# Rows of 1024 bytes in place of 520 in the expert queue of a transformer block

## The reference

```python
mod = (_silu(L0_c) @ L0_wmod).reshape(L0_c.shape[0], 6, 1, -1)
sa, ca, ga, sb, cb, gb = ...                       # ga, gb: sign kept, size at least 0.25
h = _layernorm(x) * (1 + ca) + sa
x = x + ga * attention(h, ...)                     # 16 heads, low-rank q/k/v, rope, causal
h = _layernorm(x) * (1 + cb) + sb
normed = _rmsnorm(h, norm_weight)
probs = softmax(normed @ router_weight.T)          # 8 experts
topk_w, topk_idx = jax.lax.top_k(probs, 2)         # weights divided by their sum
for e in range(8):
    gate, up = split(normed @ gate_up_weight[e].T) # 352 each
    moe_out += combine[..., e, None] * ((silu(gate) * up) @ down_weight[e].T)
x = x + gb * (h + alpha * moe_out)
```

## Time and profile before

| | |
|---|---|
| Median of 3 runs | 481.54 us (478.94 to 485.37) |
| The profiled execution | 481.55 us, span 479.7 us |
| Busy: TensorE, VectorE, ScalarE, POOL | 77%, 65%, 55%, 51% of the span |
| Bytes moved | 59.20 MB, 123 GB/s over the span |
| First stage | until about 271 us |
| Between the stages | about 271 to 285 us |
| 71 blocks | about 285 to 447 us |
| End | about 447 to 480 us |

### The profile page before, as it was taken

One profiled execution on the slowest core, in us unless ns is written; L12 is line 12 of the kernel. 1 busy time (PEld: TensorE's weight loads), 2 busy tenths in 40 slices (PEclk: granted clock), 3 DMA queues, 4 the chain that ended last, 5 costly groups with the idle time before them and its releaser, 6 DMA issues.

```text
span 479.7 us, 12085 instructions
## 1 busy us (share of the span) xinstructions
PE 368.7 (77%) x3935; PEld 300.4 (63%) x3936; DVE 310.2 (65%) x928; ACT 265.9 (55%) x467; POOL 245.1 (51%) x306
## 2 busy tenths in 40 slices
PE   3718899988897998988874119999999999999000
PEld 1416666665565656655552118999999999999000
DVE  2606899987788988988995714555454544454293
ACT  1326787876677877766662125656565565565000
POOL 3010346675577666866878721444444444344363
PEclk9967999997999899999986559999999999999655
DMA  8365656656656566665860033221221221211493
GB/s 267 74 138 143 161 145 160 173 155 155 145 122 142 153 164 154 160 154 149 266 264 33 29 100 103 65 65 51 69 55 51 66 64 42 65 52 50 120 305 105
DMA packets 56014, 59.20 MB, mean 123 GB/s; under 512 B 7167, under 2 KB 48128, under 8 KB 55712
## 3 DMA queue, kind: packets, MB, share of 16 engines
q1 hardware_dynamic: 51648, 50.15, 40.6%
q0 software_dynamic: 4320, 8.47, 5.3%
HBM read 34.81 MB, written 24.23 MB: 123 GB/s over the span
## 4 chain that ended last, share of the span: by engine, by line
PE 41%; SPq 19%; DVE 12%; DMA 11%; issue 8%; POOL 4%; another core or an unknown queue 3%; ACT 2%; POOLq 0%; DVEq 0%; ACTq 0%
PE SC L626 21%; DMA qdram<-rope 6%; SPq L366 5%; PE FB L640 5%; PE BK L640 5%; SPq L346 3%; SPq L361 3%; SPq L376 3%; PE SC L477 2%; POOL queue L1111 2%; SPq L369 2%; PE OB L499 2%; DVE pt L1038 2%; DVE pt L846 2%
## 5 line engine op out<-in xcount | busy, mean ns | idle before, releaser
L1131 POOL DMA_INDIRECT ydram<-ysb,xb x71 | 69.7, 982 | 98.5 <-DVE ysb L1024 97.2
L659 ACT ACTIVATE pt<-SC 128x1536 f32<-128x1536 f32 x64 | 92.6, 1447 | 43.6 <-PE SC L477 27.2
L626 PE MATMUL SC<-xTs,wgu 128*128 128x128 f32 x852 | 109.6, 279 | 3.9 <-issue 2.6
L626 PEld LDWEIGHTS SC<-xTs,wgu 128*128 128x128 f32 x852 | 102.0, 194 | 5.9 <-issue 5.7
L846 DVE SCALAR_TENSOR_TENSOR pt<-pt,cst 128x1024 f32<-128x1024 f32 x64 | 78.7, 1229 | 14.8 <-ACT pt L659 14.6
L477 PE MATMUL SC<-stq,stk 24*128 24x256 f32 (+1 forms) x1024 | 65.0, 364 | 26.7 <-ACT pt L659 14.8
L1111 POOL DMA_INDIRECT queue<-pl,dest x64 | 69.6, 1088 | 21.0 <-issue 20.2
L477 PEld LDWEIGHTS SC<-stq,stk 24*128 24x128 f32 x1024 | 50.0, 195 | 42.8 <-issue 18.2
L760 ACT ACTIVATE wgu<-gu,ws 128x704 f32 x71 | 62.1, 875 | 19.3 <-issue 19.1
L767 ACT ACTIVATE sg<-SC 128x384 f32<-128x384 f32 x71 | 34.8, 490 | 60.2 <-PE SC L626 53.6
L499 PE MATMUL OB<-pt,va 128*32 128x256 f32 (+1 forms) x1024 | 62.8, 350 | 5.4 <-DVE pt L848 3.1
(11 more groups left out here) (148 smaller groups left out, 590.8 us busy)
## 6 DMA issues: line engine op xcount, KB each, us to landing
stk<-kdram SPq DMA_DIRECT2D x64, 96.0 KB
stq<-qdram SPq DMA_DIRECT2D x64, 96.0 KB
xb<-queue SPq DMA_DIRECT2D x71, 65.0 KB
kdram<-rope SPq DMA_DIRECT2D x32, 128.0 KB
qdram<-rope SPq DMA_DIRECT2D x32, 128.0 KB
bc<-modrow SPq DMA_DIRECT2D x16, 256.0 KB
pt<-ydram SPq DMA_DIRECT2D x16, 256.0 KB, 5.0
gu<-gup SPq DMA_DIRECT2D x1, 2816.0 KB
```

The costliest lines, as they stand in the source:

```text
L626: last = mm(GUB[b[1] % 2][:, n, c * P:(c + 1) * P], wgu[:, b[1] % 2, n, c * P:(c + 1) * P], xTs[:, b[1] % 2, :], start=True, stop=True)
L659: af(pt[:, j, :, 0:S + P], SC[:, :, 0:S + P], ACT.Exp, scale=SCALE).then_inc(s["exp_done"], 1)
L1131: G.indirect_dma_start(ydram, bass.IndirectOffsetOnAxis(xb[:, slot(b), D + 1:D + 2].bitcast(u32), 0), ysb[:, slot(b), :], None, bounds_che ...
```

## The change

A row of the queue gets 256 numbers, 1024 bytes. Everything that has a row's width changes with it: the queue in HBM, `pl`, `xb`, and the last columns of `cst`, which hold a block of padding. The transfers that move rows are the same in number and place and move whole rows of 1024 bytes. The 126 numbers behind the first 130 are never used; in `pl` they are set to zero once, by one more instruction of POOL.

```diff
-PAYW = D + 2
+PAYW = 2 * D
...
             G.memset(wgu[:, :, :, HID:HW], 0.0).then_inc(s["z_wgu"], 1)
             G.memset(va[:, :, :, :], 0.0).then_inc(s["z_va"], 1)
+            G.memset(pl[:, :, :, :, D + 2:PAYW], 0.0).then_inc(s["z_pl"], 1)
             pool.wait_ge(s["z_va"], 1)
+            pool.wait_ge(s["z_pl"], 1)
             for hf in range(2):
```

More of the change, by code:

```diff
@@ L188, in adaln_kernel @@
         names = """cst_in x_in0 x_in ws_in wm_in w_in bc_in0 bc_in1 modrow_out dummy_out
-            z_va z_half bf_ready fold_done fold_ready st6_ready shift1_ready mv1_ready rstd1_ready
+            z_va z_pl z_half bf_ready fold_done fold_ready st6_ready shift1_ready mv1_ready rstd1_ready
             sil_ready mod_done modt_ready
```

## The result

The changed kernel took 490.13 us (median of 4 runs, 487.53 to 493.7), the kernel before 483.15 us in the same comparison (4 runs, 478.94 to 485.37): a ratio of 1.022, interval 1.0168 to 1.0272. The wide rows cost 2.2%, where +0.2% was forecast with a range up to 488. In two later comparisons, on two other chips, the loss was 3.1% and 2.9%.

The account below looks back on a forecast made before the run. TensorE was taken to bound the 71 blocks, transfers as much as engines (by the chain) the first stage, a single string between. 481.55 + 0.1 + 0.5 + 0.25 + 0.1 gave 482.5 us, range 478.5 to 488.

Parts of the forecast that it names:

- The scatters: First stage: 64 wider scatters, no extra POOL time, +0.8 us of engine time a step, +0.5 us over the whole stage.
- 1.9 us of slack: First stage: `stq` lead of 5.44 us less the worst-case 3.50 us, set against 0.8 us of scatters a step.
- Two engines nearly full, the transfers at 0.67: 180 to 240 us: TensorE busy 52.2 and VectorE 53.2 of 60 us, transfer engines 0.67 of the time.
- A: First stage: transfers bind at SP's string in each step; slower, +5.8 us (487.4) to +10.8 (492.4); chance 0.11.
- price by shares: First stage: scatters are 8.2% of the engines' time; if doubled, the 71 us stretch by that, +5.8 us, 487.4.
- 39.5%: First stage: share of its stretch that the chain gives `qdram<-rope` and SP's lines together, 71 us of the 180.
- B: POOL's scatters: POOL pays for each 512 bytes, 0.96 to 1.9 us a scatter; slower, +25 us, 507; chance 0.02.
- C: First stage scatters: whole parts are cheaper than odd 520-byte rows; faster, -5.8 us, 475.8; chance 0.07.
- count of beats: Row transfers: 520 bytes are 17 to 24 beats, 1024 aligned are 32; factor 1.33 to 1.9, load +0.09 to +0.26 us.
- Between the stages: Last scatter to first block: scatters hidden with 1.2 us to spare, first load 1.83 to 2.03-2.11 us; +0.25 taken.
- The other loads: Blocks: other 70 loads, tight only behind five to seven table readings; +0.1 us, 1.5 if all late by 0.25.
- The start: Start: clearing `pl` (0.89 us) and wider constants hidden, 0; ninth padding before the first `kdram` transfers, +0.1 us.

Follow-up runs that it names:

- b0_before: The kernel before, unchanged, run once more for a trace on the same chip as the traced changed kernel: 471.0 us (one run).
- a0_changed: The changed kernel (rows of 256 numbers) again, traced on another chip, against the kernel before: 485.12 us, ratio 1.0312.

## Why the prediction was wrong, point by point

- **The scatters** are the step that failed. The working gave them +0.5 us; the first stage grew by 6.35 us in the profiled pair and by 12.8 in the pair `b0_before` and `a0_changed`. Their price in engine time was right: +0.17 us each (0.380 against 0.207), within the +0.20 given.
- What was wrong is the weighing of slack. 1.9 us of slack at one load were set against 0.8 us of a step. But a string that runs through without a pause passes its delay on to the next step, and slack is used up once, not anew in each step. In that very trace SP's next transfer (L356) was issued at 191.15, 0.1 us after the load of `stq` that I measured at the earlier trace rows. Over the sequences 5 to 15 the lead of `stq` over the scores was 5.4 to 9.2 us before and is 2.3 to 4.1 after; the pauses of SP, 0.6 us a step in the mean, are gone too. With both used up, the step went from 14.14 only to 14.60 us. SP's string by itself, without the pauses, went from about 13.5 to 14.6, by as much as in the other pair, where nothing was left to use up. That fits the 6.35 us that the change cost here and the 12.8 there.
- **"Two engines nearly full, the transfers at 0.67"** was read as room for the transfers. The share is a mean over 16 engines and over the gaps of a serial string; with the wider rows the share of that stretch is 0.65, no higher than before, and the step grew instead.
- **The rival that came true is A**, with its place and mechanism. The changed kernel's chain is SP's string, `stq` and `bc` are waited for in eight and twelve steps. Its price by shares, +5.8 us, 487.4, is near the 6.35 us of the stage, but by luck: it has no slack that is used up first. Its upper price, every step paying 0.83 us, is the mechanism as it was; a step paid about 1.1 us, and the +10.8 compare with the 12.8 of the other pair. The 0.11 for it was too little. The chain had said 39.5%, and I held one measured lead against it.
- **B and C** are out: L1113's median is 962 ns as before, and the scatters of 1024 bytes a row cost what their bytes say. C's idea, that row ends cost something, was true only of the paddings with 1020 bytes, where nobody had put it.
- **The Trainium skill's count of beats** gave a load +0.09 to +0.26 us of engine time (Trainium skill, "DMA: Bandwidth & Descriptors", "How a descriptor splits into AXI transactions"). Within 306 to 406 us the loads took 21.4% for 47, 0.455 us each, +0.17. The measured factor, 1.59, lies inside its 1.33 to 1.9 and below the 1.97 by bytes; scatters went by 1.84.
- **Between the stages** +0.25 was given, +1.08 measured. The first load was sized rightly, 1.83 to 2.06 us, and no wait for the scatters arose. The missing term is the table reading, below.
- **The other loads:** TensorE waited once more for a block, 0.4 us, against +0.1.
- **The start:** the clearing of `pl` took 0.94 us (0.89 given) with 11.99 us of POOL's idle time left behind it. The constants landed 7.4 us after their issue in place of 7.0; hidden. The first scores started 0.34 us later, against +0.1.

## What to carry over

Before calling a transfer hidden, look whether the queue that issues around it ever waits for an engine's work. If it issues back to back through a whole period of the loop, it is a bound, and what is added to it or to the transfer engines behind it counts in each period, whatever the mean share says. A lead seen in one step is a stock and not an income: divide it by the delay a period to see how many periods it lasts. And look at more than one trace: the kernel before had a lead of 5.4 to 9.2 us in one and of 2.1 to 3.1 in another.

## What the runs showed of the hardware

- The reading of the table from SBUF by SP, right behind eight padding transfers, slowed with their size, though it reads nothing of them: 2.13 us before, and in the chain of the changed kernel

```profile
285.42 2.77 SPq L408
...
290.54 2.06 DMA xb<-queue
```

In the other traces it was 1.84 to 2.08 us with rows of 130 numbers, 2.25 with 192, 2.81 with 255, 2.71 to 2.97 with 256 and 3.69 with 384, and 2.25 and 2.26 where only the scatters were wide. So it goes mainly with the paddings' bytes (and not with their time in the engines, which at 255 numbers was 1.6 times that at 256), and it lies on the path.
- An issue on SP can be held up: L356 takes 0.35 us, L366 up to 3.7 in the pair above, 2.78 us in the mean beside scatters of 520 bytes a row and 3.31 beside those of 1024. Taking the issue ahead of it away moves the hold-up to the next one. That transfers already under way are the cause is my reading; no view names it.
- Padding writes of 1020-byte rows took 0.64 us of the engines each, of 1024-byte rows 0.40, of 1536-byte rows 0.56; scatters in the first stage didn't show this (0.353 against 0.357 us), and loads little of it (23.1% against 21.8% of 100 us in the blocks).
- Eight rows of a scatter go as one packet at 512 and 520 bytes a row and as two at 768, 1020 and 1024; the time followed bytes.
